# The adjacency half of a two-step graph layer as R(hA + R(hB)), with both products with R in the second top-p step

## What is computed

```python
def _top_p_attention(X, W1, W2, W3):
    q = X @ W1.T @ W2.T
    k = X @ W3.T
    probs = jax.nn.softmax(q @ k.T / TAU, axis=-1)
    # keep the largest probabilities of a row until they sum to TOP_P = 0.9
    ...
    return A / jnp.maximum(A.sum(-1, keepdims=True), 1e-12)
R = S + jnp.eye(N)
R = R / R.sum(-1, keepdims=True)
Xf = X
Xa = X
for n in range(2):
    A = _top_p_attention(Xa, W1, W2, W3)
    Xf = R @ Xf
    Xa = A @ Xa
    Z = Z + Xf @ U1[n].T + Xa @ U2[n].T
h = X + Z        # then a layer norm
```

## Time and profile before

| | |
|---|---|
| median of 3 runs | 952.34 us (950.48 to 953.94) |
| the profiled execution | 953.93 us |
| its span, first to last instruction | 952.2 us |
| busy: TensorE products | 709.8 us (75%) |
| busy: VectorE | 685.6 us (72%) |
| busy: ScalarE | 472.9 us (50%) |
| busy: GpSimd | 217.0 us (23%) |
| chain that ended last | VectorE 34%, TensorE 25%, ScalarE 3% |
| TensorE's mean granted clock | 0.861 |
| step 1 of L1_gnn | 335 to 536 us of the span |
| step 2 of L1_gnn | 536 to 870 us of the span |

### The profile page before, as it was taken

The page is one execution under the profiler, slowest core; times in us unless marked ns, Lnnn a source line. Parts: engine busy times, 40 slices in busy tenths (PEclk is TensorE's granted clock), DMA queues, the critical chain, the costliest instruction groups (busy, mean ns, idle before and its releaser), DMA issues.

```text
span 952.2 us, 14582 instructions
## 1 busy us (share of the span) xinstructions
PE 709.8 (75%) x4703; PEld 525.2 (55%) x4703; DVE 685.6 (72%) x2347; ACT 472.9 (50%) x691; POOL 217.0 (23%) x475
## 2 busy tenths in 40 slices
PE   4999998789994467999998871377477576557284
PEld 2555554469993334877887650166365365457153
DVE  6758678614543778777662279999999999994868
ACT  4777776125552153544445195386585685701141
POOL 3302231506664500000000031131432422500000
PEclk9999999679997578999999895597797797789588
DMA  9663000258884100000000000000000003001001
GB/s 164 98 99 56 17 24 6 90 140 233 236 233 138 38 1 1 1 2 1 1 2 1 1 1 0 1 2 1 1 1 1 1 1 90 0 3 28 0 1 44
DMA packets 50433, 41.86 MB, mean 44 GB/s; under 512 B 7376, under 2 KB 48208, under 8 KB 50352
## 3 DMA queue, kind: packets, MB, share of 16 engines
q1 hardware_dynamic: 33136, 21.00, 8.1%
q0 software_dynamic: 11456, 14.62, 7.5%
q10 hardware_dynamic: 5760, 5.27, 2.3%
HBM read 39.69 MB, written 9.57 MB: 52 GB/s over the span
## 4 chain that ended last, share of the span: by engine, by line
DVE 34%; PE 25%; ACT 3%; issue 3%; DVEq 1%; SPq 0%; DMA 0%; ACTq 0%
PE bank L1812 6%; PE bank L1866 6%; PE bank L1825 5%; DVE big L1399 4%; DVE rm L1231 4%; DVE cand L1330 3%; PE bank L1849 3%; DVE hacc L1325 2%; DVE big L1390 2%; DVE big L1387 2%; DVE cand L1348 2%; DVE top L1343 2%; ACT big L1680 1%; ACT big L1653 1%; PE bank L2006 1%
## 5 line engine op out<-in xcount | busy, mean ns | idle before, releaser
L1680 ACT ACTIVATE big<-bank 128x512 f32<-128x512 f32 x128 | 70.5, 595 | 95.0 <-PE bank L1849 94.7
L1849 PE MATMUL bank<-ident,big 128*128 128x128 f32 x512 | 81.4, 309 | 35.5 <-DVEq L1422 28.5
L1812 PE MATMUL bank<-kk,qq 64*128 64x512 f32 x256 | 80.8, 760 | 35.4 <-ACT big L1653 35.4
L1849 PEld LDWEIGHTS bank<-ident,big 128*128 128x128 f32 x512 | 62.9, 156 | 61.9 <-DVEq L1422 29.2
L1653 ACT ACTIVATE big<-bank,negm 128x2048 f32<-128x2048 f32 x32 | 62.7, 1960 | 68.9 <-DVE fsc L1426 51.2
L1129 POOL TENSOR_SCALAR bt<-bt 128x1 f32<-128x1 f32 x16 | 3.1, 194 | 364.5 <-ACT big L1670 224.1
L1399 DVE SCALAR_TENSOR_TENSOR big<-big,st 128x2048 f32<-128x2048 f32 x32 | 73.9, 2347 | 14.4 <-PE bank L1849 14.4
L365 POOL DMA_INDIRECT ys_scratch<-big,parts x62 | 60.1, 969 | 48.5 <-ACT big L720 38.4
L794 PE MATMUL bank<-big,xn 128*128 128x512 f32 x128 | 62.2, 608 | 5.7 <-DVE big L512 5.7
L778 PE MATMUL bank<-xnT 128*128 128x512 f32 x128 | 62.9, 617 | 2.3 <-DVE xnT L501 2.3
L1812 PEld LDWEIGHTS bank<-kk,qq 64*128 64x128 f32 x256 | 27.1, 228 | 66.8 <-ACT big L1653 42.4
(11 more groups left out here) (344 smaller groups left out, 1615.4 us busy)
## 6 DMA issues: line engine op xcount, KB each, us to landing
big<-in_L_ffn_w_dram SPq DMA_DIRECT2D x93, 128.0 KB
big<-in_adj_dram POOLq DMA_DIRECT2D x8, 512.0 KB, 7.4
big<-xs_scratch ACTq DMA_DIRECT2D x31, 132.0 KB
kk<-in_adj_dram POOLq DMA_DIRECT2D x4, 512.0 KB, 8.2
qq<-in_adj_dram POOLq DMA_DIRECT2D x4, 512.0 KB, 10.0
big<-ys_scratch SPq DMA_DIRECT2D x8, 256.0 KB, 4.9
xs_scratch<-hacc SPq DMA_DIRECT2D x9, 132.0 KB
xs_scratch<-hacc ACTq DMA_DIRECT2D x8, 132.0 KB
```

The source lines that it names most:

```text
L1680: nc.scalar.activation(MT[:, 4 * q:4 * q + 4, s * P:(s + 1) * P], bank[:, 5 + q % 2, :].rearrange("p (j i) -> p j i", j=4), ACT.Copy).then ...
L1812: nc.tensor.matmul(bank[:, c, :], qq[lo:lo + DA, (g * G + s) * P:(g * G + s + 1) * P], kk[lo:lo + DA, c * CH:(c + 1) * CH], start=True, st ...
L1849: mm = nc.tensor.transpose(bank[:, 5 + q % 2, j * P:(j + 1) * P], mk[:, s, jt * P:(jt + 1) * P], ident[:, :])
```

## The change

1. **The products with the weights come first.** `make_ab(q)` multiplies chunk q of h with both matrices of the adjacency half, four products of 256 columns, at the start of step 1. ScalarE copies hA into `hacc` and the first part of hB (`take_ab`), VectorE takes the rest (`rest`), ScalarE the second part (`second`), VectorE the third (`third`). This takes the place of splitting h (`split`, `split2` and two ScalarE copies of 2048 columns).
2. **No product with R in step 1.** The eight `rx(0, g)` of 48 products go from it.
3. **The inner product, R(hB), stands at the head of step 2.** It is made as `rx(1, g)` was (96 products of 128 columns): three calls between the logits of the first tiles, five in the first group. VectorE adds each to hA (`take_w`, two instructions a call).
4. **The sum w = hA + R(hB) is split with TensorE.** `less_w(half, j)` makes w minus the parts so far in PSUM, with the identity and with minus the identity (`negb`); ScalarE rounds it to the next part (`take_part`). There are three such rounds for each half of the rows.
5. **The outer product, R w,** is made two calls to a group in the groups of index 2 to 5 (`RXG`), where there was one call in each of the indices 1 to 7 and one at the end. `add_up` becomes `add_pv` and `add_rx`.
6. The adjacency products between the steps (two of the four `u_quad`) and all of `xf_quad` go. The adding of the identity to adjT on GpSimd moves behind the layer norm of h. Two pairs of semaphores become one.
7. `low` of the first group of step 2 is half of `mk` and not `hacc`, since hA lies there. The second group waits before it writes `low` until the last `less_w` is through (`sp_done` at 12).

The flag product stands behind both products with the values, as before; in the groups of index 2 to 5 a call of `rx` stands between them.

The diff, cut to its core:

```diff
 # VectorE
-                def add_up(g):
+                def add_pv(g):
...
+                def add_rx(g):
+                    dve.wait_ge(rx_done, NG + g + 1)
...
+                def take_w(g):
+
+                    dve.wait_ge(rx_done, g + 1)
+                    dve.wait_ge(ab_part, 2 * NC)
+                    for s in range(G):
+                        t = g * G + s
+                        nc.vector.scalar_tensor_tensor(out=hacc[:, t, :], in0=bank[:, RB[g % 2], s * P:(s + 1) * P],
+                                                       scalar=rinv[:, t:t + 1], in1=hacc[:, t, :],
+                                                       op0=ALU.mult, op1=ALU.add).then_inc(w_done, 1)
...
+                    if n and g == 0:
+                        lowg = mk[:, 1, :]
+                        dve.wait_ge(tq_done, gg * 4 * G)
+                    if n and g == 1:
+                        dve.wait_ge(sp_done, 12)
...
                 row_max(0, 0, 0)
-                split()
+                rest(0)
                 row_max(0, 0, 1)
-                split2()
+                third(0)
+                rest(1)
                 row_max(0, 1, 0)
+                third(1)
+                for q in range(2, NC):
+                    rest(q)
+                    third(q)
...
                 for p in range(2):
                     xa_quad(p)
+                take_w(0)
                 row_max(n, 0, 1)
                 for p in range(2, NC):
                     xa_quad(p)
+                take_w(1)
                 row_max(n, 1, 0)
-                for p in range(NC):
-                    xf_quad(p)
+                take_w(2)
 # ScalarE
+                take_ab(0)
                 exp(0, 0, 0)
...
+                take_ab(1)
+                second(0)
                 exp(0, 0, 1)
+                take_ab(2)
+                second(1)
...
+                    if g == 0:
+                        take_ab(3)
+                        second(2)
+                        second(3)
...
                     if g + 1 < NG:
                         exp(1, g + 1, 0)
+                    if g == 1:
+                        take_part(1, 0)
                     if g:
                         for k in range(4 * G):
                             copy_MT(1, g - 1, k)
+                            if g == 1 and k == 1:
+                                take_part(1, 1)
+                                take_part(1, 2)
...
+                    if g == 0:
+                        for j in range(3):
+                            take_part(0, j)
 # TensorE
+                def less_w(half, j):
...
+                    for i in range(2):
+                        q = 2 * half + i
+                        if j:
+                            pe.wait_ge(sp_part, 6 * half + 2 * (j - 1) + i + 1)
+                        mm = nc.tensor.matmul(bank[:, WB[half][i], :], ident[:, :],
+                                              hacc[:, q * TPC:(q + 1) * TPC, :].rearrange("p t d -> p (t d)"), start=True,
+                                              stop=(j == 0))
+                        for k in range(j):
+                            mm = nc.tensor.matmul(bank[:, WB[half][i], :], negb[:, :],
+                                                  parts[:, k, q * TPC:(q + 1) * TPC, :].rearrange("p t d -> p (t d)"),
+                                                  start=False, stop=(k == j - 1))
+                        mm.then_inc(sp_done, 1)
...
                     if g < NG:
                         flag_sum(g)
-                    if g + 1 < NG:
-                        rx(0, g + 1)
...
+                    if g == 1:
+                        less_w(1, 1)
                     if g + 1 < NG:
                         logits(1, g + 1, 1)
+                    if g == 1:
+                        less_w(1, 2)
                     if g:
                         turn_mk(1, g - 1, range(2, 8))
-                        if g < NG:
-                            rx(1, g - 1)
+                        for k in range(0, NG, 2):
+                            if RXG[k] == g:
+                                rx(1, k)
                         pv(1, g - 1, 0)
+                    if g == 0:
+                        for k in range(3, 6):
+                            rx(0, k)
                     if g + 2 < NG:
                         logits(1, g + 2, 0)
+                    if g == 0:
+                        for k in range(6, NG):
+                            rx(0, k)
+                        for j in range(3):
+                            less_w(0, j)
                     if g:
                         pv(1, g - 1, 1)
+                    for k in range(1, NG, 2):
+                        if RXG[k] == g:
+                            rx(1, k)
                     if g < NG:
                         flag_sum(NG + g)
+                    if g == 0:
+                        less_w(1, 0)
```

More of the change, by code:

```diff
@@ L1294, in add_up @@
                     dve.wait_ge(pv_done, G * (gg + 1))
-                    dve.wait_ge(rx_done, gg + 1)
-                    for s in range(G):
-                        v = op(nc.vector.scalar_tensor_tensor(
-                            out=h[:, g * G + s, :], in0=bank[:, 4, s * P:(s + 1) * P],
-                            scalar=rinv[:, g * G + s:g * G + s + 1], in1=h[:, g * G + s, :], op0=ALU.mult, op1=ALU.add))
-                    since(v)
+                    if not PV_FIRST[g]:
+                        dve.wait_ge(rx_added, G * (g + 1))
                     for s in range(G):
@@ L1367, in group @@
                     dve.wait_ge(tq_done, gg * 4 * G)
+                    if n and g == 0:
+                        take_w(5)
+                    for k in range(0, NG, 2):
+                        if n and RXG[k] == g:
+                            add_rx(k)
                     if n:
@@ L1411, in group @@
                         row_max(n, g + 2, 0)
+                    if n and g == 0:
+                        take_w(7)
                     if n and g:
-                        add_up(g - 1)
+                        add_pv(g - 1)
+                        for k in range(1, NG, 2):
+                            if RXG[k] == g:
+                                add_rx(k)
                     dve.wait_ge(flags_sum, gg + 1)
@@ L1733, in _ @@
                     take_u(p)
+                act.wait_ge(c_id, NT + 1)
                 below(0, 0, 0)
@@ new lines, in less_w @@
+                def less_w(half, j):
+                    if j == 0:
+                        pe.wait_ge(w_done, NT if half else NT - G)
+                        pe.wait_ge(u_act, NC)
+                        pe.wait_ge(u_dve, NC)
+                        if half:
+                            pe.wait_ge(sp_part, 6)
+                        else:
+                            pe.wait_ge(c_id, NT + 1)
+                    for i in range(2):
+                        q = 2 * half + i
+                        if j:
[8 more added lines that the diff above has]
+                        mm.then_inc(sp_done, 1)
```

249 lines of the change are left out of this document (133 added, 116 removed).

## The result

The changed kernel takes **955.67 us** (median of 9 runs, 954.69 to 959.4), the kernel before on the same chip 951.12 (9 runs, 947.64 to 953.94): a ratio of **1.0046 [1.0032, 1.0061]**. It is slower by 4.5 us; 946.8 us and "faster" had been predicted, and the time lies above the upper end of the range, 953. The profiled execution took 956.58 us with a span of 954.8, against 953.93 and 952.2 before.

What follows compares the result with a forecast made beforehand. TensorE was taken as the bound in step 1, VectorE busier at the head of step 2. The terms -20.4 + 7.5 + 12.5 - 5.1 gave -5.5 us, from 952.34 to 946.8 us, range 940.0 to 953.0.

Steps and rivals of the forecast that it cites:

- A group of step 1: Step 1: without the 48 products a group takes 17.9 us, 3.4 less; six groups give -20.4 us.
- the slow first group: First group of step 1: transposes and logits may run at half clock after an idle stretch, 2 us taken.
- The prediction's own sign of being wrong: Step 1: the forecast is wrong if groups take over 19 us.
- rival 4: Step 1: the clock falls in each group's 1.3 us gap; 959 us with 2 us each; chance 0.03.
- The start: Start of step 1: later first group and transposes, +7.5 us (4.1 to 9.7), including 2 for half clock.
- The head: Head of step 2: late flags and a new wait for the last `less_w`, +12.5 us (+11 to +17).
- rival 3: Head of step 2: TensorE at half clock, some 17 us more, 964 us; chance 0.08.
- The tail: End of step 2: the last transposes no longer follow the last `rx` call, -5.1 us (-4 to -6).
- The middle: Rest of step 2: two `rx` calls a group in four groups cost 0 us, bounds -1 to +2.
- Rival 1: Seams cost nothing: the start costs 1 and not 7.5 us, 940.3 us; chance 0.15.
- Rival 2: All bounds costly: start +9.7, groups gaining 3.2, head +15; no change, 952.7 us; chance 0.15.
- Rival 5: Step 1: some wait keeps the old order, groups stay at 21.3 us; chance part of Rival 2's.

Runs made afterwards that it cites:

- e3: Changed kernel plus eight idle products behind the flag product and eight behind the first two transposes of each step 1 group: 0.9974 of the kernel before.
- e4: Kernel before with only the tail's edit, the last product with R made a group earlier, ahead of the last flag product: 0.9952 of the kernel before.
- e2: Changed kernel with step 1's flag product ahead of the second half of the products with the values: 0.9979 of the kernel before.
- e1: Changed kernel with `low` of step 2's second group in `xnT`, the wait for `less_w` one group later: 945.67 us, 0.9937 of the kernel before.
- e8: Changed kernel with the edits of e1, e2 and e6, plus twelve idle products behind the first two transposes of each step 1 group: 0.9847 of the kernel before.
- e5: Changed kernel with step 1's row factors computed ahead of the flags, leaving out exact recomputation of flagged rows there: 0.9907 of the kernel before.
- e9: The changed kernel, unaltered, measured again on a third chip: 1.0039 of the kernel before.
- e6: Changed kernel with `rest` and `third` of the last two chunks moved behind VectorE's first group of row maxima: 1.0052 of the kernel before.
- e11: Kernel of e3 with the later splits of e6, on the third chip: 0.9965 of the kernel before.
- e12: Changed kernel with the edits of e1 and e2 plus twelve idle products, without the later splits: 0.9861 of the kernel before.
- e10: Kernel of e3 measured again on the third chip: 0.9978 of the kernel before.

## Why the prediction was wrong

It missed by 8.1 us in the ledger (+2.6 for -5.5), and all of that, and more, lies in **"A group of step 1"**, which gained 4.6 us in place of 18.4 (with the slow first group). The prediction's own sign of being wrong, groups of over 19 us, came true: five of the six took 19.1 to 22.1.

- *The step that failed.* "From the start of the transposes to the flag product it takes 15.91 us now; 15.9 + 0.6 + 0.2 + 1.15 is 17.9 us a group." That stretch was carried over with 0.6 us for ScalarE's copy. It takes 17.77 us in a fast group (399.29 to 417.06), 1.86 more: not the third block waits (0.25 us, as before), but the logits ahead of it, 1.74 us for banks that the exponential still reads. I had the exponential's end at 437.28 in my rows, 2.75 us after VectorE goes on at 434.53, where the first transposes take 1.04: that gives a wait of 1.7 us. I asked only who waits for ScalarE's copies. The instruction between the first and the second transposes has a wait of its own; in the kernel before it was met by then. Fast groups so take 19.1 to 19.4 us: with 1.26 more than the sum had in each of six, 7.6 us are explained.
- *The second half of the miss is rival 4*, with a chance of 0.03: the clock falls in step 1. Three groups of the profiled run took 2.6 us more than their neighbours, 7.8 us, of which I had 2 in the sum for the first. e3 shows the price: 7 us in the ratio. With 7.6 and 5.8 (7.8 less 2), 13.4 of the 13.8 us are accounted for. The rest is of the size by which the waits for `m_ready` differ: from the flag product to the transposes it is 1.66 and 1.62 us in the first two of these groups and 1.3 in the others, where 1.35 was in the sum.
- *Why rival 4 had so small a chance.* The argument against it was that a gap of 2.17 us left the products fast, 2.19 us. That reading was luck. e4 has the same instructions there, and the same sixteen products behind the same gap took 3.35 us:

```profile
562.86 3.35 PE L1958 MATMUL bank<-UT,hacc 128*128 128x128 f32 x16 [2.17 <-DVE xn L1468]
```

The changed kernel shows it again: the logits behind a gap of 2.41 us at the head of step 2 took 1.99 us (571.67), but 3.58 and 3.45 us in e2 and e3, whose step 2 is the same. And it does not take two gaps a group: in e2 the first is 0.24 us or gone, and logits behind 1.87 us took 3.60. What decides whether the clock falls behind a given gap stays open; that it sometimes does should have had more than 0.03.
- *Behind rival 4* I named the Trainium skill (TensorE: Matmul & The Clock Gate, "HAM oscillation — how this bites in real kernels"). The page's loop begins every round slowly, and the wait in it is longer than the products of a round. The trace agrees in kind only: an idle gap and then slow products, but in three groups of six, and in two of these behind gaps of under 2 us. So the page's example did not price this case either, and the measurement decides.
- *The start* was over-costed: +3.3 for +5.5. VectorE's first group started 6.2 us later within step 1 (360.56 - 334.31 against 355.09 - 335.04), where 7.0 had been the low end. The cover was as predicted: 6.2 less the 0.9 and the 2 us of slack is 3.3. What was too high is the middle that I took between full and half clock, since the logits ran at full clock there (1.99 us at 343.00, 349.75 and 356.49), behind gaps of 2.8 to 3.1 us. This is not to be relied on: the same logits took 3.24, 1.99 and 3.66 us in e3, whose idle products come only later.
- *The head* was right in mechanism and place: the wait at L1369 is 9.90 us (9.5 predicted), the calls of `rx` ran at full clock (5.52 us each at 544.70 and 556.35, 16.25 for three at 573.59), rival 3 did not come, flags were read at +75.2 (77.0 predicted) and the stretch costs 10.3 for 12.5. e1 shows that 8.3 us of it are this wait.
- *The tail* was right: -4.9 for -5.1, and e4 shows the same gain by itself, 4.6 us. *The middle* of step 2, at nothing, was right to 0.01 us.
- Rival 1 fell. Rival 2 gave 952.7 us, with start and head dearer than they were; it was short in the groups alone, where its 3.2 us stand against 0.8 on average (4.6 / 6). Rival 5 fell: every instruction moved as written.

So in all, the change removes 5.4 us a group from the busiest engine, but 1.1 to 1.5 and 1.74 us of that turn into waits at once, and three groups of six run in part at the lower clock: the first behind the long gap at the start, the others behind these waits. What is left pays for the start of step 1, and the head of step 2, where the shared buffer `hacc` adds a wait of 9.9 us, makes the kernel slower. With the buffer moved, the flag product earlier, the clock held and two chunks split later, the same change is 1.5% faster than the kernel before (e8). About 0.5% of that is the tail's edit, which needs nothing else of the change (e4).

## What to carry to other kernels

When work is taken from the engine that is the bound, list every wait of each instruction behind the gap, the reuse of a PSUM bank included, with the time at which it was met before: each one that was met under the removed work becomes a wait now. A cheap producer of an answer (a flag product) goes ahead of work that hides the round trip, and a buffer borrowed across engines is priced by its last reader. Where short gaps come back every round, price the clock too, and take no single row as proof that a gap is harmless: look for the same place in a second profile. Try idle products in the gap before giving up on the change.

## What was not expected of the hardware

- Gaps of 1.1 to 1.5 and 1.74 us per group of some 19 us, with TensorE busy 83% of the time, went with a granted clock of 0.93 over the middle of step 1: logits then ran at the lower level (1.2 GHz) in some groups, 3.78 us for 1.99. In e2 one gap of 1.74 to 1.88 us was enough (busy 88%, clock 0.95). With waits of 0.86 and 0.82 us (e5, busy 89%) and with fillers (e3, busy 93%) it stayed 1.00.
- Which products are slow is not fixed by the code. Of the six groups there are three in the first profile and five in e9, which is the same kernel; sixteen products behind a gap of 2.17 us took 2.19 us before and 3.35 in e4. While the clock moves like this, an edit of 2 us is hard to judge in this kernel (e6, e11, e12).
- Sixteen idle products of 256 columns a group, about 2.1 us of TensorE's time, cost nothing that shows and gave back 6 to 7 us by the ratios (e3 on one chip, e10 beside e9 on another).
